# Attention and mixture-of-experts kernel: the last batch's heads in a buffer of their own, their scaling ahead of the slots, the row table ahead of the expert table

## The reference, cut to what matters

```python
logits = xf @ Wr / temp
topw, topi = jax.lax.top_k(logits, TOP_K)
topw = jax.nn.softmax(topw, axis=-1)
for e in range(NUM_EXPERTS):
    h = xf @ W1[e] + b1[e]
    a, g = jnp.split(h, 2, axis=-1)
    y = a * jax.nn.silu(g) @ W2[e] + b2[e]
    we = jnp.sum(jnp.where(topi == e, topw, 0.0), axis=-1, keepdims=True)
    out = out + y * we
```

## Time and profile before

| | us |
|---|---|
| median of 3 runs | 1049.57 |
| lowest, highest | 1048.76, 1050.04 |
| the profiled execution | 1049.65 |
| its span (first to last instruction) | 1047.8 |
| PE busy in the span | 958.1 (91%) |
| DVE busy | 782.6 (75%) |
| ACT busy | 555.0 (53%) |
| POOL busy | 508.1 (48%) |

### The profile page before, as it was taken

How to read it: one execution, slowest core, us unless ns; L and a number is a source line. 1 busy time by engine, 2 the same in 40 slices (tenths; PEclk the granted TensorE clock), 3 DMA queues, 4 the chain that set the end, 5 groups by cost and what they waited for, 6 DMA issues and landing times.

```text
span 1047.8 us, 21901 instructions
## 1 busy us (share of the span) xinstructions
PE 958.1 (91%) x5804; PEld 574.1 (55%) x5805; DVE 782.6 (75%) x2291; ACT 555.0 (53%) x1202; POOL 508.1 (48%) x972
## 2 busy tenths in 40 slices
PE   4999899999999999999989956299999999999993
PEld 2444243333333333333345546288888888888883
DVE  3675999999999999999966556466766666676762
ACT  1555067777777777777763535143433334434431
POOL 5555536666666666666633745543322323233232
PEclk9999589999999999999997966599999999999998
DMA  3688966485867867644456588753555375333332
GB/s 98 215 266 213 234 137 153 93 257 99 257 153 216 250 156 209 150 90 89 89 149 184 188 217 275 224 161 52 140 134 131 50 210 136 55 50 56 54 51 35
DMA packets 107729, 156.53 MB, mean 149 GB/s; under 512 B 26944, under 2 KB 82240, under 8 KB 105088
## 3 DMA queue, kind: packets, MB, share of 16 engines
q1 hardware_dynamic: 83696, 128.03, 45.8%
q0 software_dynamic: 13296, 17.77, 9.8%
q10 hardware_dynamic: 10656, 9.78, 3.5%
HBM read 90.46 MB, written 64.69 MB: 148 GB/s over the span
## 4 chain that ended last, share of the span: by engine, by line
PE 78%; DVE 8%; DMA 5%; ACT 3%; issue 2%; POOL 1%; ACTq 1%; SPq 0%; DVEq 0%; POOLq 0%
PE bank L860 13%; PE bank L881 13%; PE bank L842 13%; PE bank L2020 6%; PE bank L2022 6%; PE bank L2021 6%; PE bank L2050 3%; PE bank L2052 3%; PE bank L2051 3%; PE bank L2034 3%; PE bank L1632 2%; DMA e_rows<-slot_rows 2%; DVE a_xn L314 2%; PE a_ckv L363 2%; PE bank L1996 1%
## 5 line engine op out<-in xcount | busy, mean ns | idle before, releaser
L816 ACT ACTIVATE b_prob<-bank 128x512 f32<-128x512 f32 (+3 forms) x768 | 311.9, 507 | 79.7 <-PE bank L860 78.9
L842 PE MATMUL bank<-b_k_st,b_q_st 96*128 96x512 bf16 (+3 forms) x768 | 255.6, 346 | 5.8 <-DVE b_neg_max L770 1.7
L770 DVE CUSTOM_DVE_ANT_0 bank<-bank,b_mask_max 128x256 f32<-128x256 f32 (+3 forms) x512 | 241.6, 510 | 22.2 <-PE bank L842 22.0
L860 PE MATMUL bank<-b_q_st,b_k_st 99*128 99x512 bf16 (+3 forms) x768 | 242.9, 334 | 4.0 <-ACT b_prob L816 2.0
L726 POOL TENSOR_SCALAR_AFFINE_SELECT b_prob<-b_prob 128x128 f32<-128x128 f32 x512 | 147.0, 300 | 188.5 <-ACT b_prob L816 184.2
L1846 POOL DMA_INDIRECT out_dram<-e_y,e_token x71 | 110.5, 1557 | 238.6 <-issue 158.0
L773 DVE TENSOR_REDUCE b_neg_max<-bank 128x1 f32<-128x512 f32 x256 | 175.8, 687 | 13.4 <-PE bank L842 11.2
L881 PE MATMUL bank<-b_prob,b_v_aug 128*32 128x512 f32 (+3 forms) x1536 | 146.3, 500 | 0.0
L842 PEld LDWEIGHTS bank<-b_k_st,b_q_st 96*128 96x128 bf16 x768 | 75.9, 99 | 109.3 <-DVE b_neg_max L770 52.1
L860 PEld LDWEIGHTS bank<-b_q_st,b_k_st 99*128 99x128 bf16 x768 | 74.8, 99 | 106.3 <-ACT b_prob L816 79.1
L2020 PE MATMUL bank<-w_ring,e_rowsT_hi 128*128 x284 | 125.3, 441 | 3.5 <-DVE e_rowsT_lo L1871 2.2
(11 more groups left out here) (203 smaller groups left out, 1470.7 us busy)
## 6 DMA issues: line engine op xcount, KB each, us to landing
w_parts<-w_ring SPq DMA_DIRECT2D x10, 1536.0 KB, 7.3
w_ring<-w_parts SPq DMA_DIRECT2D x10, 1024.0 KB, 7.6
e_rows<-slot_rows ACTq DMA_DIRECT2D x74, 129.0 KB, 2.1
w_raw<-in_L_ffn_W SPq DMA_DIRECT2D x8, 1024.0 KB, 5.2
ctx_cols<-b_ctx_out SPq DMA_DIRECT2D x16, 512.0 KB
q_parts<-a_part_q SPq DMA_DIRECT2D x8, 768.0 KB, 4.0
k_parts<-a_part_k SPq DMA_DIRECT2D x8, 768.0 KB, 4.8
b_q_st<-q_parts SPq DMA_DIRECT2D x16, 384.0 KB, 5.0
```

The costliest lines, as they stand in the source:

```text
L770: nc.vector.tensor_tensor_reduce(scores, scores, mask_max[:, HALF - width:HALF], -1.0, -MASKED, ALU.add, ALU.min, to).then_inc(max_done, 1)
L816: nc.scalar.activation(prob[n % NP][:, 0:width], prob_ps[n % NS][:, 0:width], ACT.Exp, scale=SCALE).then_inc(prob_ok, 1)
L842: nc.tensor.matmul(out[:, 0:width], q_st[g % RING][0:STACK, h, i * P:(i + 1) * P], k_st[g % RING][0:STACK, h, half * HALF:half * HALF + wi ...
L860: nc.tensor.matmul(prob_ps[n % NS][:, 0:width], k_st[g % RING][0:MAXROWS, h, j * P:(j + 1) * P], q_st[g % RING][0:MAXROWS, h, q0:q0 + widt ...
```

## The change

There are four edits, all in the routing and its handover to the experts.

1. The heads of batch 3 get a buffer of their own in slot 3 of the weight ring. Its load no longer waits for a projection, and it is issued right behind `load_den(3)`, ahead of the store of the inverses.
2. On SP, a wait for the last scale transfer is put ahead of `store_x2(2)`.
3. On DVE, `scale_heads(3)` moves from behind `slots(1)` to in front of it.
4. In `tables`, the four operations that make the row table move up, the reduction writes one partition in place of 128, into `fresh`'s memory read as floats, and a semaphore of its own (`tile_row_ok`) tells ACT that this table is there. `fresh` becomes the last table. PE turns tile 0 before it waits for `tables_ok`.

```diff
@@ Route.__init__
+        self.last_heads = weights.raw[:, W_STAGES, 0, 0:DC * SEQ].rearrange("p (c n) -> p c n", c=DC)
...
+        self.jumped = self.fresh[:].bitcast(F32)
...
+        self.tile_row_ok = sem("r_tile_row_ok")
...
+    def heads_of(self, b):
+        return self.heads[:] if b < BATCH - 1 else self.last_heads
+
     def load_heads(self, sp, b):
-        if b:
+        if 0 < b < BATCH - 1:
             sp.wait_ge(self.proj_ok, b * PAIRS)
...
@@ Route.sync
         self.load_den(sp, 3)
+        self.load_heads(sp, 3)
         self.store_inverse(sp, 3)
         self.load_scale(sp, 3)
-        self.load_heads(sp, 3)
         self.load_x(sp, 3)
+        sp.wait_ge(self.scale_in_ok, 16 * DC * BATCH)
         self.store_x2(sp, 2)
...
@@ tables, behind the first reduction (line 1487)
+            then(nc.vector.tensor_tensor(passed[:], passed[:],
+                                         self.jump[:].unsqueeze(1).to_broadcast([P, TABLE, SEGMENTS]),
+                                         ALU.mult))
+            then(nc.vector.tensor_reduce(self.jumped, passed[0:1], AX.X, ALU.add))
+            then(nc.vector.tensor_tensor(same[:], self.row_of_tile[:], self.jumped, ALU.add))
+            then(nc.vector.tensor_scalar(self.tile_row[:], same[:], float(EXPERTS * REGION), None, ALU.min))
+            dve.sem_inc(self.tile_row_ok, 1)
...
@@ tables, the end (lines 1502 to 1509)
-            then(nc.vector.tensor_scalar(self.fresh[:], same[:], -16.0, 16.0, ALU.mult, ALU.add))
-            then(nc.vector.tensor_tensor(passed[:], passed[:],
-                                         self.jump[:].unsqueeze(1).to_broadcast([P, TABLE, SEGMENTS]),
-                                         ALU.mult))
-            then(nc.vector.tensor_reduce(tile_f[:], passed[:], AX.X, ALU.add))
-            then(nc.vector.tensor_tensor(same[:], self.row_of_tile[:], tile_f[0:1, :], ALU.add))
-            nc.vector.tensor_scalar(self.tile_row[:], same[:], float(EXPERTS * REGION), None,
-                                    ALU.min).then_inc(self.tables_ok, 1)
+            nc.vector.tensor_scalar(self.fresh[:], same[:], -16.0, 16.0, ALU.mult, ALU.add).then_inc(self.tables_ok, 1)
...
@@ DVE's order
         choose(1)
+        scale_heads(3)
         slots(1)
         filled_by_two()
-        scale_heads(3)
         shift(2)
...
@@ expert phase, ACT
-        act.wait_ge(route.tables_ok, 1)
+        act.wait_ge(route.tile_row_ok, 1)
...
@@ expert phase, PE
+        rows_turned(0, 0)
         pe.wait_ge(route.tables_ok, 1)
-        rows_turned(0, 0)
```

More of the change, by code:

```diff
@@ L1110, in load_scale @@
                 self.scale_in_ok, 16)
+    def heads_of(self, b):
+        return self.heads[:] if b < BATCH - 1 else self.last_heads
     def load_heads(self, sp, b):
-        if b:
+        if 0 < b < BATCH - 1:
             sp.wait_ge(self.proj_ok, b * PAIRS)
         context = self.dram["ctx"].rearrange("g (q s) n -> s (g q) n", s=2)[0]
-        sp.dma_start(self.heads[:], context[b * D:(b + 1) * D, :].rearrange("(c p) n -> p c n", p=P)).then_inc(
+        sp.dma_start(self.heads_of(b), context[b * D:(b + 1) * D, :].rearrange("(c p) n -> p c n", p=P)).then_inc(
             self.heads_in_ok, 16)
@@ L1311, in scale_heads @@
         def scale_heads(b):
+            heads = self.heads_of(b)
             dve.wait_ge(self.heads_in_ok, 16 * (b + 1))
@@ L1316, in scale_heads @@
                 half = slice(k // DC * CHUNK, (k // DC + 1) * CHUNK)
-                nc.vector.tensor_tensor(self.heads[:, k % DC, half], self.heads[:, k % DC, half],
+                nc.vector.tensor_tensor(heads[:, k % DC, half], heads[:, k % DC, half],
                                         self.scale[:, k % DC, half], ALU.mult).then_inc(self.heads_ok, 1)
@@ L1632, in project @@
                 last = self.nc.tensor.matmul(self.project_bank(b, t)[:, i * D:(i + 1) * D],
-                                             self.heads[:, c, (2 * t + i) * P:(2 * t + i + 1) * P],
+                                             self.heads_of(b)[:, c, (2 * t + i) * P:(2 * t + i + 1) * P],
                                              self.wo[:, c, :], start=(c == 0), stop=(c == DC - 1))
```

## The result

| | us |
|---|---|
| after, median of 9 runs | 1052.89 |
| lowest, highest | 1051.34, 1056.66 |
| before, median of 9 runs beside it | 1049.29 |
| ratio, 95% interval | 1.0041, 1.0028 to 1.0054 |
| profiled execution of after, its span | 1053.15, 1051.2 |

The change makes the kernel slower by 0.41%, some 4 us, where I forecast 3.6 us faster. The interval of the ratio lies clear of 1. In the two profiles shown the spans differ by 3.4 us, and the following splits those.

What follows compares the result with a forecast made beforehand. PE was taken to bound the expert stage at full clock, so an earlier start ends the program earlier. Scaling 3.5 us earlier, less a 1.7 us scatter wait, plus 1.8 from tables gave 3.6 us: 1046.0, range 1042.3 to 1049.0.

Steps and rivals of the forecast that it cites:

- so I take the landing of the heads, 602.9: Store of batch 3's inverses: queued behind the heads, it lands with them at 602.9, 0.9 us after the old scale issue.
- I take the middle, 9.7: Batch 3's scale transfer: takes 9.7 us, between 7.7 and 11.6, so scaling starts at 614.5, 3.5 us earlier.
- second rival: Batch 3's scale takes 11.6 us or more whatever surrounds it; gain about 1.0 to 1.7 us, 1048.3; chance 0.2.
- first rival: Batch 3's scale is undisturbed by what is queued behind it: 7.70 us, gain 5.6 us, 1044.0; chance 0.2.
- the first rule: DMA queue: descriptors consumed in order per engine, so nothing issued behind the scale could delay it; sum 5.6 us.
- Nothing, as forecast: SP's wait for the scale: holding back x2 and pad stores costs nothing; bias loads run from 637.4 to about 643.
- the new wait of 1.7 us: ACT's rows of batch 3 wait 1.7 us for the late scatter, ends 0.4 and 3.4, whenever scaling starts.
- what it waits for besides landed long before: ACT's first row loads at the handover: nothing but the row table holds them, so its 1.8 us counts.
- the 1.8 us in the sum: Routing tables: the row table is ready at 664.3 instead of 666.13, counted as 1.8 us of gain.
- From tile 0 on all distances are as before: Expert stage: after tile 0 starts, all distances stay unchanged, with no further gain or loss.
- 3.5 - 1.7 + 1.8 = +3.6: Whole sum: earlier scaling 3.5, less ACT's scatter wait 1.7, plus earlier row table 1.8, gives 3.6 us faster.
- The third rival: normalise(3) on ACT waits for the scatter behind a scaling at 620.2; slower, 1053.4; chance 0.07.

Runs made afterwards that it cites:

- e1: Changed kernel with x's load for batch 3 issued behind SP's wait for the scale instead of ahead of it; ratio to before 1.0016.
- e7: Before plus only the early heads load of batch 3 and SP's wait for the scale; ratio to before 1.0002.
- e10: Changed kernel with the store of batch 3's inverses issued ahead of the heads load; ratio to before 1.0002.
- e8: Changed kernel with slots ahead of scaling, inverses' store ahead of heads, x behind SP's wait, y_ok raised right behind the row table; ratio to before 0.9974.
- e4: Changed kernel with y_ok raised right behind the row table, ACT waiting for all tables before copying tile 0; ratio to before 1.0040.
- e5: Changed kernel with slots(1) put back ahead of the scaling of batch 3; ratio to before 1.0010.
- e12: Changed kernel with an unused Silu on ACT ahead of its row-table wait, so ACT's table load runs early; ratio to before 1.0030.
- e15: Changed kernel timed once more, unaltered, on the slower chip; ratio to before 1.0030.
- e17: The kernel of e12, changed kernel with the early Silu, timed once more; ratio to before 1.0033.
- e13: The kernel of e8 plus the early unused Silu on ACT, on the slower chip; ratio to before 1.0001.
- e18: The kernel of e13 timed once more; ratio to before 1.0006.
- e16: Before with only the scaling of batch 3 moved ahead of slots(1) on DVE; ratio to before 1.0025.
- e3: Before with only the row table first, its own semaphore, and PE turning tile 0 before it waits; ratio to before 0.9987.
- e11: Before with the row table first and y_ok raised right behind the row table; ratio to before 0.9985.
- e14: Before with the early unused Silu on ACT, on the slower chip; ratio to before 1.0002.
- e19: The kernel of e14, before with the early Silu, timed once more; ratio to before 0.9995.

## Why the prediction was wrong, point by point

**Edit 1, "so I take the landing of the heads, 602.9".** The mechanism held, the store waits behind the 1 MB that was issued ahead of it: 5.45, 4.81 and 5.13 us behind the heads (after, e1, e7), 1.55 and 2.43 ahead of them (e10, e8). The Trainium skill, "DMA: Bandwidth & Descriptors", section "Queues, rings and completion order", has descriptors of one queue consumed in order on each engine, and these rows agree: in after the heads land 7.7 us after 596.21, at 603.9, and the store behind them at 604.94. It was sized too small: I had both at 602.9, so the store landed 2.0 later than I took, half of it because the heads themselves were 1.0 late.

**Edit 1, "I take the middle, 9.7".** With the store's 2.0 this is the term that failed. Between the scale's issue and the scaling I had 11.6 us; it took 13.1 (604.95 to 618.04), so 11.2 by the count that had 9.7. x alone beside the scale is enough for nearly the whole disturbance, and undisturbed it took 9.2 by the same count in e1 (11.1 less 1.6 and 0.3), not the 7.7 of batch 2. (The 7.70 us were a window in which the scale moved by itself; batch 2's scale had been issued at 565.65, 10.05 us before the end of that window at 575.70, of which my count explains 9.3.) With store and scale together the scaling was 19.5 us behind the inversion, not 15.1: 2.0 us for the store and 1.5 for the scale, and 3.5 us of gain became nothing (618.04), or a loss of 1.0 by the ruler. Nearest to it was my second rival, "the heads were hidden behind the scale anyway"; e7 is its case by itself, 1.0002. But it had 616.4 to 617, and its reason was a scale that takes 11.6 us "whatever surrounds it", which e1 refutes: without x it took 9.2.

**The rule that spoke for the first rival.** From the scale's issue until SP, which waits for it, goes on, it took 11.0 us in e1 and 10.4 in e8 with nothing behind it, 12.8 to 13.2 with x behind it (after and the six runs with its order: e4, e5, e7, e12, e15, e17), 16.2 in e10 with the heads right ahead and x behind. On the slower chip it took 13.8 and 12.7 with the heads right ahead and nothing behind (e13, e18), so x is not all that can draw it out; what the heads add there, or the chip, these runs do not separate. The rule of order in one queue, of the same section of the Trainium skill, would have let nothing behind the scale hold it up. In e1 the scale alone was moving at a share of 0.46 to 0.48, thus on half of the engines. The measurements decide against the use that I made of the first rule: in e1 against after only x's place differs, so what is queued behind shares something with the scale, even if not its engines' order. What it shares these runs do not show.

**Edit 2.** Nothing, as forecast. The bias loads, which I had from about 643, went from 646.7; no engine is seen waiting for them.

**Edit 3, the new wait of 1.7 us.** Confirmed in place and cause in the profiles of the first two chips that have edit 3, 1.28 against 1.7 in after; in those of the slower chip ACT's rows do not wait for it. But I argued that it did not depend on when the scaling starts and subtracted it from a gain. Without that gain all that is left of edit 3 is its cost. e5 and e16 show it from both sides: 3 us gone by undoing it, 2.7 us lost by doing it alone. Of these the wait explains 1.3 in after's trace, and the first tiles 0.7 (16.53 against 15.87 in e5). It isn't always so dear: e10 has edit 3 and ACT's wait for the scatter too (2.98 us idle), and is level with before.

**Edit 4, "what it waits for besides landed long before".** The tables' part was right, 1.9 us against 1.8. The sentence on ACT was wrong, and with it the 1.8 us in the sum: I looked at the transfers it waits for, and not at `y_ok`, a plain semaphore that DVE raises only after the last table. e3 and e4 show that this, and only this, held the load.

**What no step had: the clock.** "From tile 0 on all distances are as before" failed by 1.35 us. The profiles of the first two chips in which PE waited 1.7 to 2.3 us for the first gated hidden (after, e4, e8, e11) show 16.5 us from tile 0 to the second turn and a clock down to 0.50; those with 0.8 to 1.4 us show 15.0 to 15.3, and 15.9 in e5, with no fall. The slower chip agrees: a fall behind 1.72 and 2.04 us (e15, e16), none right behind 0.69 us or less (e12, e13, e14, e17, e18, e19). Shortening the wait removed the fall at that place (e12 against e15). So the fall goes with the wait in all the profiles; that it costs 1.35 us is read from after's profile alone, for the runs of after with a short wait (e12, e17) were no faster than after.

**The sum.** Forecast 3.5 - 1.7 + 1.8 = +3.6; measured 0 - 1.3 + 0, less 1.35 for the clock and some 0.8 of small shifts: -3.4 in the two profiles. The third rival, slower, had the right place (the wait for the scatter behind a late scaling) and needed a scaling at 620; without edit 4's gain it needed no such delay.

There is also a next bound behind these. In e1, with tile 0 at 671.59, PE stood still for 1.6 us near 695, because tile 6's load waits for the last batch's second scatter: POOL starts the last of those eight at 688.74, and ACT issues that load at 693.60, inside 4.41 us in which it does nothing else.

No run moved that scatter, so what it costs in the faster version stays open. So does the larger part of edit 3's cost on the slower chip, and why before itself takes 20 us longer there.

## What to carry to other kernels

Work that fills a hole is not free to move: before it is put behind a wait, follow its own output to the next reader of the buffer, and count the move as a loss unless the wait really ends earlier. When a transfer is the last to land, removing it shows the next one, and what is queued with that one sets its time: hold back loads that aren't needed yet, and put small stores that others wait for ahead of large loads. And when a semaphore is moved forward, read every wait between it and the first instruction it is meant to release.

## What was not expected of the hardware

- A load that kept half of the DMA engines busy (share 0.46 to 0.48) was slowed by a load queued behind it: 1 MB of scale was there 11.0 us after its issue with nothing behind it (e1) and 13.0 with x behind it (after). With the heads just ahead it took 10.4 on one chip and 12.7 to 13.8 on another, and 16.2 with x behind as well.
- In the six profiles in which PE waited 1.68 to 2.27 us for the first gated hidden, some 3 us at 1.2 GHz followed; in after they cost 1.35 us. So a gain of one or two us ahead of such a wait can be returned entirely, as in e11. On the first two chips PE waited the longer, the sooner its clock had risen behind tile 0's first product: 0.82 us with the rise 6.0 us behind it (e7), 2.27 with the rise 3.2 behind it (e4).
- The same kernel takes 1049.7 and 1050.0 us on two chips and 1069 us on a third. There the traces give waits of ACT of 3.4 to 10.7 us to something off the core (14 us in all between 624 and 640 in e19, before with the early Silu), where before's trace on a faster chip has a wait of 6.37 us for PE; and ACT's issue of the first three row loads takes up to 11.6 us, against 4.4 to 5.1 on the others.
